# Value tiles of 125 or 128 rows, stored to DRAM and loaded again, in a decoder layer

## The chip, the cores and the metric

The kernel runs on one core of a Trainium2 chip. A core has five engines with instruction queues of their own: TensorE (PE), VectorE (DVE), ScalarE (ACT), GpSimd (POOL) and SyncE (SP), which here issues nearly all DMAs. They work on one on-chip memory of 128 partitions (SBUF, called `big` in this kernel) and wait for each other by semaphores. Transfers between SBUF and DRAM are carried out by 16 DMA engines. The metric is the time of one execution on the device in microseconds (us). The runs agree within about 0.3%.

## The reference

A decoder layer with pre-norm on a batch of 8 sequences of 112 tokens, width 512, and a context of 375 tokens per sequence:

```
x1  = x + self_attention(norm(x))                 16 heads of 32, rotary, causal mask
z   = ln(norm(x1))
S   = gqa(ln(q(z)), ln(k(z)), v(z))               16 query heads, 8 key/value heads of 128
X   = gqa(ln(qx(z)), ln(kx(ctx)), vx(ctx))        kx, vx: 512 -> 1024, from the 375 context tokens
x2  = x1 + fp8(concat(S, X)) @ wproj              inputs of q, k, v, qx and wproj rounded to fp8
h   = silu(gate(norm(x2))) * up(norm(x2))         2048 wide, ternary weights
out = x2 + rms_norm(h) @ w_proj                   ternary weights
```

The part that matters here is `vx(ctx)`: the values of the cross attention, for each of the 8 sequences a matrix of 375 x 1024. The 375 context tokens are worked on in three chunks of 125 tokens, and a chunk's tokens lie on 125 of the 128 partitions.

## The kernel before

The program has four layers of work that overlap: the first layer (self attention, up to about 200 us), two halves of the fp8 self attention (`S0`, `S1`), two halves of the cross attention (`X0`, `X1`, from 446 to 992 us), and the gated MLP. Each engine's order is written out by hand: a table of ticks (`A_PLAN` for the first layer, `ORDER` and `ORDER_X` for the rest) says which stage of which batch an engine issues at each tick. Every engine works strictly in that order, SP's DMA issues included.

To fill TensorE in the first layer, a part of the cross attention's work is done early. For each of 24 chunks of context (8 batches, 3 chunks each; `v_ld`, `v_in`) the split into two bf16 parts is made, and the result is stored to DRAM as `cs` (`v_cs`). For the first chunk of each batch (`EARLY = (0,)`) the value product is made as well, in two halves `h` of 512 columns: `v_mm` on TensorE (L1071), the copy out of PSUM into `v_out[h]` on ACT (`v_ev`, L1363), and the store from there to DRAM as `vs` (`v_st` on SP, L989). That makes 16 stores of 125 rows of 2 KB. `v_out[h]` is free again for the next copy when its store has landed.

On SP these stores stand between others: `cs` stores (L983), loads of context and of weights into one of four staging buffers (L941; `in_w_s` are the weights of the `S` halves, each load 512 KB over 128 rows), and the first layer's sum of a batch, which goes to DRAM and comes back in other rows (`xs`, L959 and L968). ACT takes a staged weight when it has landed (`b_0`, L1465).

In the cross attention, each of 16 steps (two halves, 8 batches) loads its value tile from `vs` into `vX[b % 2]` (`p_mm` on SP, L1018), as soon as the attention of the batch two before it is finished. The products of the attention weights with the values (`t_s3`, L1205) wait for it. They contract over 125 rows.

Lines that the text below names: on ACT L1397 the exponentials of the first layer and L1408 the copy of the transposed weights, L1503 the normalised projections; on VectorE L1744 the scaled output of a batch's attention; on TensorE L1059 the first layer's projections, L1121 its products with the values, L1081, L1109 and L1093 transposes and masks, L1144 and L1151 the projections of the halves.

Of the kernel before, what the change touches and what calls it, by code (L numbers as in the profile page):

```python
# [16 lines left out]
CK = 125  # L17
# [134 lines left out]
EARLY = (0,)  # L152
# [234 lines left out]
def _program(nc, ctx, x, ctx_t, w_a, w_s, w_x, w_v, w_p, w_g, w_d, vec, bias, cst, cst2, scr, xs, cs, vs, out):  # L387
# [4 lines left out]
    def sem(name):  # L392
        return ctx.enter_context(nc.semaphore(name))

    def signal(name, *stages, if_=None, each=None):

        keys = [k for s, k in steps["table"] if s in stages and (if_ is None or if_(k))]
        return Signal(sem("s_" + name), keys if each is None else [(k, e) for k in keys for e in each])

    def f32(a, n):  # L400
        return big[:, a:a + n]
# [79 lines left out]
    v_out = [f32(early.take(512), 512) for _ in range(2)]  # L481
# [12 lines left out]
    vX = [f32(a, 1536).rearrange("p (c n) -> p c n", c=3) for a in (X_V0, X_V1)]  # L494
# [24 lines left out]
    def unit(u):  # L519

        name, i = u
        n, c = divmod(i, 4)
        if name == "F":
            src = w_g[n // 2, :, n % 2, :] if n < 8 else w_d[n - 8]
            return src[:, 1024 * (c // 2):1024 * (c // 2) + 1024], None, None, None
        src, psrc = {"S": w_s, "X": w_x}[name[0]][int(name[1])], w_p[HALVES.index(name)]
        rows = src[n] if n < 4 else psrc[n - 4]
        rows = rows[:, 1024 * (c // 2):1024 * (c // 2) + 1024]
        if n >= 4:
            h = 4 * (n - 4) + c  # L530
            return rows, wp_half[name][:, 0, h, :], wp_half[name][:, 1, h, :], None
        sl = slice(512 * c, 512 * c + 512)
        v = ((0, 1, 2) if name[0] == "S" else (3, None, None))[max(0, c - 1)]
        scale = None if v is None else wsc[:, 4 * v + n:4 * v + n + 1]
        return rows, w_half[name][:, 0, n, sl], w_half[name][:, 1, n, sl], scale
# [6 lines left out]
    def spilled(u):  # L542
        return u[0] == "F" and u[1] >= FFN_DIRECT
# [22 lines left out]
    def att_no(h, b, g=3, e=1):  # L566
        return ATT.index((h, b, g, None if h[0] == "S" else e))
# [8 lines left out]
    def is_v(n):  # L576
        return PROJ[n][2] == "v"

    def proj_before(h, b):

        if b:
            return last_no(h, b - 1, "kv")
        return last_no("X0", NB - 1, "kv") if h == "X1" else proj_no("S1", NB - 1, "v", 0)

    def x_free(h, b, last):

        nb = NB * (h == "X1") + b
        if nb == 0:
            return [p_sum[proj_no("S1", NB - 1, "v", 0)]]
        if nb == 1:  # L590
            return [pv[att_no("S1", NB - 1)]]
        hb = divmod(nb - 2, NB)
        return [last[att_no(HALVES[2 + hb[0]], hb[1])]]
# [22 lines left out]
    s_vs = [Signal(sem(f"s_vs{i}"), [k for k in V_MADE if k[1] == i], 16) for i in range(2)]  # L616
    x_batches = [(h, b) for h in HALVES[2:] for b in range(NB)]
    s_ctx = Signal(sem("s_ctx"), x_batches, 16)
    s_vx = [Signal(sem(f"s_vx{i}"), [k for k in x_batches if k[1] % 2 == i], 16) for i in range(2)]
# [85 lines left out]


    pool_step = Steps(sem("s_pool_step"))
    rotated = signal("rotated", "a_rot")
    negmean = signal("negmean", "p_rstd", if_=lambda n: not is_v(n))
    q_made = Signal(sem("s_q_made"), quants("POOL", "t_s4"))  # L710
# [221 lines left out]
    def ps(user):  # L932
        return psum[bank.of[user]][:, :]

    def sync_program(e):
        w = Waits(e)

        def stage_load(user, n, src):
            for free in stage.after[user]:
                w.wait_ge(*free)  # L940
            e.dma_start(stage_buf[stage.of[user]][:, 0:n], src).then_inc(s_st[stage.of[user]], 16)  # L941

        def prep_a(c):
            for k in range(4):
                e.dma_start(wa_in[4 * c + k], w_a[k, :, 768 * c:768 * c + 768]).then_inc(s_wa[4 * c + k].sem, 16)
            if c == 0:
                e.dma_start(x1[0:T, 1, :], x[1]).then_inc(s_x[1].sem, 16)
                return
            e.dma_start(a_bias[0:T, :], bias).then_inc(s_bias.sem, 16)
            e.dma_start(vc, vec).then_inc(s_vec.sem, 16)  # L950
            e.dma_start(ck, cst2).then_inc(s_vec.sem, 16)
            for b in range(2, NB):
                e.dma_start(x1[0:T, b, :], x[b]).then_inc(s_x[b].sem, 16)

        def a_s4(g):
            b = g // 4
            if g % 4 == 3:
                w.wait_ge(*x1_made[g])
                e.dma_start(xs_rows[T * b:T * b + T, :], x1[0:T, b, :]).then_inc(s_xs[b].sem, 16)  # L959

        def l_h(b):
            i = b - 1
            if b:
                w.wait_ge(*s_xs[i]["out"])
                w.wait_ge(*s_xs[b]["out"])
                w.wait_ge(*stats["l_ln", i])
                w.wait_ge(*zl_made[i])
                e.dma_start(x1t[:, i, :], xs_rows[128 * i:128 * i + 128, :]).then_inc(s_xl[i].sem, 16)  # L968

        def b_0(u):  # L970
            if u[1] % 2 == 0:
                stage_load(u, 1024, unit(u)[0])

        def v_w(i):
            if i % 2 == 0:
                stage_load(("v_w", i), 1024, w_v[i // 2])

        def v_ld(m):
            stage_load(("v_ld", m), 1000, ctx_t[m])

        def v_cs(n):
            w.wait_ge(*chunk_lo[n])
            e.dma_start(cs[n // 3, :, n % 3, :], chunk_words[V_BUF[n]]).then_inc(  # L983
                s_cs[V_BUF[n]].sem, 16)

        def v_st(k):
            n, h = k
            w.wait_ge(*v_made[k])
            e.dma_start(vs[h, n // 3, :, EARLY.index(n % 3), :], v_out[h][0:CK, :]).then_inc(s_vs[h].sem, 16)  # L989

        def b_4(u):
            if spilled(u):
                w.wait_ge(*t_made[u])
                e.dma_start(scr[u[1] - FFN_DIRECT], spill_buf[spill_slot.of[u]]).then_inc(spill_out[u][0], 16)

        def b_back(_):
            for i in range(4):
                w.wait_ge(s_sp[i], 16 * sp_nth[i])
            w.wait_ge(*p_out[att_no("X0", 7)])
            for j in range(N_BACK):  # L1000
                e.dma_start(f32(PW[1] + 256 * (FFN_DIRECT + 4 * j), 1024).rearrange("p (u w) -> p u w", u=4),
                            scr[4 * j:4 * j + 4].rearrange("u p w -> p u w")).then_inc(s_back.sem, 16)

        def p_mm(n):
            h, b, what, c = PROJ[n]
            if h[0] == "S":
                return
            if (what, c) == ("q", 0):
                for s in s_cs:
                    w.wait_ge(*s[max(s.value)])  # L1010
                w.wait_ge(*p_sum[proj_before(h, b)])
                e.dma_start(ctx_words, cs[b].rearrange("p c w -> p (c w)")).then_inc(s_ctx.sem, 16)
            if (what, c) == ("k", 2):
                for s in s_vs:
                    w.wait_ge(*s[max(s.value)])
                for free in x_free(h, b, pv):
                    w.wait_ge(*free)
                e.dma_start(vX[b % 2][0:CK, 0:len(EARLY), :], vs[int(h[1]), b]).then_inc(s_vx[b % 2].sem, 16)  # L1018

        def d_1(b):  # L1020
            w.wait_ge(*y_out[b])
            e.dma_start(out_rows[128 * b:128 * b + 128, :], x1t[:, b, :]).then_inc(s_out.sem, 16)

        mine = dict(prep_a=prep_a, a_s4=a_s4, l_h=l_h, b_0=b_0, b_4=b_4, b_back=b_back, p_mm=p_mm, d_1=d_1,
                    v_w=v_w, v_ld=v_ld, v_cs=v_cs, v_st=v_st)
        for s, k in steps["SP"]:
            if s in mine:
                mine[s](k)
        e.wait_ge(*s_out[NB - 2])
# [274 lines left out]
    def scalar_program(e):  # L1304
        w = Waits(e)
# [51 lines left out]
        def v_ev(k):  # L1357
            n, h = k
            w.wait_ge(*v_sum[n, h, 2])
            before = V_MADE.index(k) - 2  # L1360
            if before >= 0:
                w.wait_ge(*s_vs[h][V_MADE[before]])
            e.activation(v_out[h][0:CK, :], ps(("v_mm", k))[0:CK, :], ACT.Copy).then_inc(v_made.sem, 1)  # L1363

        def a_rstd(b):
# [639 lines left out]
    def gpsimd_program(e):  # L2005
        w = Waits(e)
# [97 lines left out]
            e.tensor_tensor(sm[:, 1:2], sm[:, 0:1], cf[:, C_HALF:C_HALF + 1], ALU.pow).then_inc(f_rstd.sem, 1)  # L2104

        mine = dict(a_rot=a_rot, l_q=l_q, b_1=b_1, b_2=b_2, p_rstd=p_rstd, t_s4=t_s4, g_1=g_1, d_0=d_0)
        for s, k in steps["POOL"]:
            if s in mine:
                mine[s](k)
# [7 lines left out]
    @block.gpsimd  # L2117
    def _(eng):
        gpsimd_program(eng)
# [87 lines left out]
```

## Time and profile before

| | us |
|---|---|
| median of 3 runs | 1171.3 |
| lowest, highest | 1168.83, 1171.52 |
| the profiled execution | 1172.57 |
| its span in the profile | 1170.8 |

| engine | busy us | share of the span |
|---|---|---|
| TensorE | 1128.7 | 96% |
| VectorE | 836.1 | 71% |
| ScalarE | 795.0 | 68% |
| GpSimd | 608.4 | 52% |

The profile is one execution, recorded by the hardware. It tells for each instruction when it ran, which idle time of its engine lay ahead of it and what most likely ended that idle time (the releaser). The span is the time from the first to the last instruction; the execution's own time has 1.8 us more around it. "DMA share" is the mean busy share of the 16 DMA engines over a stretch: 1.00 is all sixteen at work. "PEclk" is the granted TensorE clock over a stretch, as a share of full speed. The mean over the whole span is 0.991.

### The profile page before, as it was taken

To read this page: it belongs to the slowest core of one execution; us is meant where nothing else is said; L and a number is where in the kernel's file an instruction comes from. 1 tells how busy PE (TensorE), PEld (TensorE's weight loads), DVE (VectorE), ACT (ScalarE), POOL (GpSimd) and SP (SyncE) were. 2 spreads that over 40 slices of the span, in tenths; PEclk is the share of its full clock that TensorE was granted. 3 is DMA by queue.
4 is the path that set the end of the run, shared out by engine and by line. 5 is a ranking of instruction groups with operands and counts; after the bars stand their busy time and mean duration, and the time that the engine had idled before them with its cause. 6 is when DMAs were issued, how large, how long until landed. Compare 5 with 4: busy or idle time off the path is not lost.

```text
span 1170.8 us, 20518 instructions
## 1 busy us (share of the span) xinstructions
PE 1128.7 (96%) x6269; PEld 766.3 (65%) x6330; DVE 836.1 (71%) x2761; ACT 795.0 (68%) x2348; POOL 608.4 (52%) x761
## 2 busy tenths in 40 slices
PE   5899999979999999999999999999999999999998
PEld 3576676756777776667667667667766767554564
DVE  5767997899877886668778776757776686676242
ACT  5665766888887887667777666667867678675130
POOL 1543885586454456526366464535545462356172
PEclk9999999999999999999999999999999999999999
DMA  9435433232211113023322223221341210000000
GB/s 283 161 110 177 132 111 100 67 107 73 73 55 37 38 55 108 30 96 108 117 85 77 83 88 99 72 81 37 119 139 56 90 37 10 1 1 1 36 1 27
DMA packets 36205, 92.98 MB, mean 79 GB/s; under 512 B 3568, under 2 KB 13936, under 8 KB 36096
## 3 DMA queue, kind: packets, MB, share of 16 engines
q1 hardware_dynamic: 35824, 91.30, 23.9%
q8 instruction: 51, 0.84, 0.3%
q14 instruction: 58, 0.48, 0.1%
q10 hardware_dynamic: 272, 0.36, 0.1%
HBM read 74.07 MB, written 17.58 MB: 78 GB/s over the span
## 4 chain that ended last, share of the span: by engine, by line
PE 84%; DVE 5%; DMA 4%; ACT 3%; issue 2%; SPq 1%; POOL 1%; ACTq 0%; DVEq 0%
PE ps L1151 17%; PE ps L1144 12%; PE ps L1205 8%; PE ps L1250 8%; PE ps L1221 8%; PE ps L1177 7%; PE ps L1186 4%; PE ps L1262 4%; PE ps L1163 4%; PE ps L1059 3%; DMA big<-in_w_s 2%; PE ps L1174 2%; PE ps L1071 2%; DMA big<-in_w_v 1%; PE ps L1121 1%
## 5 line engine op out<-in xcount | busy, mean ns | idle before, releaser
L1151 PE MATMUL ps<-big 128*125 128x512 bf16 x960 | 220.4, 379 | 0.0
L1503 ACT ACTIVATE big<-ps,big 112x128 f32<-112x128 f32 (+1 forms) x512 | 193.5, 465 | 15.3 <-POOL big L2061 14.5
L1144 PE MATMUL ps<-big 128*112 128x512 bf16 x768 | 187.5, 388 | 6.6 <-DVE big L1886 6.2
L1151 PEld LDWEIGHTS ps<-big 128*125 128x125 bf16 x960 | 127.5, 136 | 64.2
L1635 DVE BATCH_NORM_STATS2 big<-ps 112x6 f32<-112x128 f32 (+1 forms) x512 | 113.4, 284 | 43.9 <-PE ps L1151 28.7
L1144 PEld LDWEIGHTS ps<-big 128*112 128x112 bf16 x768 | 98.1, 132 | 60.2 <-DVE big L1886 6.8
L2058 POOL TENSOR_SCALAR big<-big 112x4 f32<-112x4 f32 (+1 forms) x128 | 46.3, 361 | 144.8 <-DVE big L1643 144.5
L1205 PE MATMUL ps<-big 125*128 125x224 f32 (+1 forms) x512 | 118.5, 353 | 1.2
L2071 POOL TENSOR_TENSOR big<-big 128x448 f32<-128x448 bf16 x64 | 62.8, 981 | 108.0 <-DVE big L1927 107.8
L1562 ACT ACTIVATE big<-ps 125x336 f32<-125x336 f32 x96 | 43.5, 453 | 103.1 <-PE ps L1186 102.6
L1205 PEld LDWEIGHTS ps<-big 125*128 125x128 f32 (+1 forms) x512 | 96.1, 191 | 13.1 <-issue 0.4
L1538 ACT ACTIVATE big<-ps,big 128x448 f32<-128x448 f32 (+1 forms) x128 | 95.0, 742 | 13.0 <-PE ps L1163 13.0
L1177 PE MATMUL ps<-big 128*112 128x375 f32 x256 | 101.7, 478 | 0.1
L1553 ACT ACTIVATE big<-ps,big 112x375 f32<-112x375 f32 x128 | 73.0, 570 | 42.2 <-DVE big L1846 42.2
L1846 DVE TENSOR_REDUCE big<-ps 112x1 f32<-112x375 f32 x128 | 68.8, 538 | 45.8 <-PE ps L1177 45.6
L1250 PE MATMUL ps<-big 128*128 128x512 bf16 (+1 forms) x505 | 98.6, 352 | 0.4
L1221 PE MATMUL ps<-big 128*128 128x512 bf16 x423 | 96.0, 379 | 1.3
L1867 DVE TENSOR_SCALAR big<-big 112x112 f32<-112x112 f32 (+1 forms) x256 | 94.9, 392 | 2.6 <-PE ps L1186 1.9
L2061 POOL TENSOR_TENSOR big<-big 112x4 f32<-112x4 f32 (+1 forms) x128 | 47.2, 369 | 82.1 <-ACT big L1314 78.2
L1186 PE MATMUL ps<-big 112*125 112x112 f32 (+1 forms) x512 | 84.3, 266 | 0.0
L1186 PEld LDWEIGHTS ps<-big 112*125 112x125 f32 (+1 forms) x512 | 73.0, 174 | 17.1 <-issue 0.4
L1250 PEld LDWEIGHTS ps<-big 128*128 128x128 bf16 x512 | 50.1, 98 | 44.4
(128 smaller groups left out, 2406.6 us busy)
## 6 DMA issues: line engine op xcount, KB each, us to landing
big<-cs SPq DMA_DIRECT2D x16, 750.0 KB, 4.2
big<-in_w_s SPq DMA_DIRECT2D x16, 512.0 KB, 4.3
big<-in_w_p SPq DMA_DIRECT2D x16, 512.0 KB, 5.2
big<-in_w_x SPq DMA_DIRECT2D x16, 512.0 KB, 3.8
big<-in_w_g SPq DMA_DIRECT2D x16, 512.0 KB, 5.3
big<-in_ctx_t SPq DMA_DIRECT2D x12, 500.0 KB, 7.1
cs<-big SPq DMA_DIRECT2D x24, 250.0 KB, 3.6
big<-in_w_d SPq DMA_DIRECT2D x8, 512.0 KB, 5.0
```

Of the source, the lines that this page charges most:

```text
L1144: t = e.matmul(bk[0:T, :], xq[:, k, :], wt[:, s, k, col:col + 512], start=k == s == 0, stop=k == 3 and s == 1)
L1151: t = e.matmul(bk[0:CK, :], ctxT[:, c, s, k, :], wt[:, u, k, col:col + 512], start=k == s == u == 0, stop=k == 3 and s == 1)
L1177: t = e.matmul(bk[0:T, 0:SC], q_sb[i][:, 2 * g + one, :], kX[i][:, g, :], start=True, stop=True)
L1186: t = e.transpose(bk[0:rows, T * j:T * j + T], p[0:T, rows * j:rows * j + rows], identf[0:T, 0:T])
L1205: t = e.matmul(ps(user)[:, o:o + 224], v[0:rows, c, 128 * g:128 * g + 128], pt[0:rows, 224 * c:224 * c + 224], start=c == 0, stop=S or c == 2)
L1221: t = e.matmul(bk, cat[:, k, :], wp_half[h][:, s, k, :], start=k == s == 0, stop=k == 7 and s == 1)
L1250: t = e.matmul(bk[:, 0:wide], wg[:, kk, 2048 * which + 128 * m:2048 * which + 128 * m + 128], xT[:, s, kk, n0:n0 + wide], start=kk == s == ...
L1503: t = e.activation(z[0:rows, 128 * j:128 * j + 128], ps(("p_mm", n))[0:rows, 128 * j:128 * j + 128], ACT.Identity, bias=v["q"][:, j:j + 1] ...
L1538: e.activation(dst, ps(("p_t", n))[:, 0:4 * rows].rearrange("p (g t) -> p g t", g=4), ACT.Identity, bias=bs, scale=wt).then_inc(qk_sb.sem, 1)
L1553: t = e.activation(p[0:T, 0:SC], bk[0:T, 0:SC], ACT.Exp, bias=sm[0:T, 0:1], accum_out=sm[0:T, 2:3])
L1635: t = e.bn_stats(v["st"][:, j, :], src[0:rows, width * j:width * j + width])
L1867: t = e.tensor_scalar(dst, src, ri[:, j:j + 1], None, ALU.mult)
```

## The change

The value tiles are stored and loaded as 128 rows in place of 125. The DRAM tensor `vs` gets 128 rows for each tile. GpSimd sets both buffers `v_out[0]` and `v_out[1]` to zero once, before all its other work, and signals it (`v_clear`). ACT waits for that signal ahead of its copy, which still writes rows 0 to 124, so rows 125 to 127 stay zero in every tile that is stored. The load writes all 128 rows of `vX`, and the products still read 125 of them. No other instruction is added, removed or moved.

```diff
--- before.py
+++ after.py
@@ -705,6 +705,7 @@
 
 
     pool_step = Steps(sem("s_pool_step"))
+    v_clear = Signal(sem("s_v_clear"), range(2))
     rotated = signal("rotated", "a_rot")
     negmean = signal("negmean", "p_rstd", if_=lambda n: not is_v(n))
     q_made = Signal(sem("s_q_made"), quants("POOL", "t_s4"))
@@ -986,7 +987,7 @@
         def v_st(k):
             n, h = k
             w.wait_ge(*v_made[k])
-            e.dma_start(vs[h, n // 3, :, EARLY.index(n % 3), :], v_out[h][0:CK, :]).then_inc(s_vs[h].sem, 16)
+            e.dma_start(vs[h, n // 3, :, EARLY.index(n % 3), :], v_out[h]).then_inc(s_vs[h].sem, 16)
 
         def b_4(u):
             if spilled(u):
@@ -1015,7 +1016,7 @@
                     w.wait_ge(*s[max(s.value)])
                 for free in x_free(h, b, pv):
                     w.wait_ge(*free)
-                e.dma_start(vX[b % 2][0:CK, 0:len(EARLY), :], vs[int(h[1]), b]).then_inc(s_vx[b % 2].sem, 16)
+                e.dma_start(vX[b % 2][:, 0:len(EARLY), :], vs[int(h[1]), b]).then_inc(s_vx[b % 2].sem, 16)
 
         def d_1(b):
             w.wait_ge(*y_out[b])
@@ -1360,6 +1361,7 @@
             before = V_MADE.index(k) - 2
             if before >= 0:
                 w.wait_ge(*s_vs[h][V_MADE[before]])
+            w.wait_ge(*v_clear[h])
             e.activation(v_out[h][0:CK, :], ps(("v_mm", k))[0:CK, :], ACT.Copy).then_inc(v_made.sem, 1)
 
         def a_rstd(b):
@@ -2104,6 +2106,9 @@
             e.tensor_tensor(sm[:, 1:2], sm[:, 0:1], cf[:, C_HALF:C_HALF + 1], ALU.pow).then_inc(f_rstd.sem, 1)
 
         mine = dict(a_rot=a_rot, l_q=l_q, b_1=b_1, b_2=b_2, p_rstd=p_rstd, t_s4=t_s4, g_1=g_1, d_0=d_0)
+
+        for h in range(2):
+            e.memset(v_out[h], 0.0).then_inc(v_clear.sem, 1)
         for s, k in steps["POOL"]:
             if s in mine:
                 mine[s](k)
@@ -2200,7 +2205,7 @@
     scr = nc.dram_tensor("scr", (36, 128, 256), mb.dt.float32, kind="Internal").ap()
     xs = nc.dram_tensor("xs", (896, 512), mb.dt.float32, kind="Internal").ap()
     cs = nc.dram_tensor("cs", (8, 128, 3, 500), mb.dt.float32, kind="Internal").ap()
-    vs = nc.dram_tensor("vs", (2, 8, 125, len(EARLY), 512), mb.dt.float32, kind="Internal").ap()
+    vs = nc.dram_tensor("vs", (2, 8, 128, len(EARLY), 512), mb.dt.float32, kind="Internal").ap()
     decoder_layer(nc, *args, scr, xs, cs, vs, out)
     r = run(nc, [{"in_" + k: v for k, v in arrays.items()}], core_ids=[0])
     return r.results[0]["out_0"]
```

The only engine whose order changes is GpSimd. Its first rows before (`big` is SBUF; the TENSOR_TENSOR rows are the rotation of queries and keys in the first layer):

```order
L2196 MEMSET const-float32-1.0 128x1
L2196 MEMSET const-bfloat16-1.0 128x1
L2196 MEMSET const-uint8-127 128x1
L2117 UNCONDITIONAL_BRANCH
L2018 ISA
L2018 TENSOR_TENSOR big<-big 112x512
L2020 TENSOR_TENSOR big<-big 112x512
L2023 TENSOR_TENSOR big<-big 112x512
```

The same place in the changed kernel (line numbers are some lines higher):

```order
L2201 MEMSET const-float32-1.0 128x1
L2201 MEMSET const-bfloat16-1.0 128x1
L2201 MEMSET const-uint8-127 128x1
L2122 UNCONDITIONAL_BRANCH
L2111 MEMSET big 128x512 x2
L2020 ISA
L2020 TENSOR_TENSOR big<-big 112x512
L2022 TENSOR_TENSOR big<-big 112x512
L2025 TENSOR_TENSOR big<-big 112x512
```

Two memsets of 128x512 now stand ahead of the first rotation; all rows behind them keep their order.

## Rows read from the trace of the kernel before

**Rows 1.** the page: busy time of the engines, and the chain that ended last

```profile
PE 1128.7 (96%) x6269; PEld 766.3 (65%) x6330; DVE 836.1 (71%) x2761; ACT 795.0 (68%) x2348; POOL 608.4 (52%) x761
...
PE 84%; DVE 5%; DMA 4%; ACT 3%; issue 2%; SPq 1%; POOL 1%; ACTq 0%; DVEq 0%
```

**Rows 2.** busy time by stage: stretch, length, each engine, TensorE clock, DMA share, GB/s

```profile
60.00:130.00 70.00, 65.77 (x453) 46.87 (x452) 50.71 (x87) 47.03 (x166) 34.28 (x26) 1.00 0.43 140
130.00:200.00 70.00, 69.78 (x495) 50.56 (x493) 59.32 (x121) 43.82 (x164) 55.06 (x46) 1.00 0.37 114
446.00:992.00 546.00, 543.90 (x2805) 381.81 (x2841) 393.19 (x1484) 392.35 (x1099) 275.87 (x378) 1.00 0.25 82
```

**Rows 3.** DMA issues by line, with landing; and the instructions that touch `vs`

```profile
vs<-big SPq DMA_DIRECT2D x16, 250.0 KB
...
cs<-big SPq DMA_DIRECT2D x24, 250.0 KB, 3.6
...
L989 SPq DMA_DIRECT2D vs<-big x16: 255/332/894, 59.8 to 204.9; - x16
...
L1018 SPq DMA_DIRECT2D big<-vs x16: 270/271/300, 446.0 to 980.5; - x16
```

**Rows 4.** narrow stretches: last store alone, a `cs` store, before a landing

```profile
205.30:208.30 3.00, 3.00 (x31) 2.38 (x30) 1.27 (x3) 2.58 (x8) 0.20 (x1) 0.82 0.32 101
146.00:147.00 1.00, 1.00 (x7) 0.58 (x5) 0.96 (x2) 1.00 (x8) 1.00 (x2) 1.00 0.81 278
123.00:124.00 1.00, 1.00 (x6) 0.60 (x5) 0.97 (x3) 0.12 (x1) 0.92 (x2) 1.00 0.34 133
```

**Rows 5.** SP's queue, 86 to 114 us: start, length, line, what is issued

```profile
86.98 0.33 SPq L989 DMA_DIRECT2D vs<-big  x1
...
87.79 0.65 SPq L941 DMA_DIRECT2D big<-in_w_s  x1
...
110.58 0.38 SPq L941 DMA_DIRECT2D big<-in_w_s  x1
...
111.95 0.39 SPq L989 DMA_DIRECT2D vs<-big  x1
...
113.83 2.87 SPq L941 DMA_DIRECT2D big<-in_w_s  x1
```

**Rows 6.** ACT timeline: its waits for `in_w_s`, idle time and releaser in brackets

```profile
82.81 0.72 ACT L1465 ACTIVATE big<-big 128x512 bf16<-128x512 f32 x1 [3.82 <-DMA big<-in_w_s]
...
96.22 0.72 ACT L1465 ACTIVATE big<-big 128x512 bf16<-128x512 f32 x1 [3.97 <-DMA big<-in_w_s]
...
114.74 0.72 ACT L1465 ACTIVATE big<-big 128x512 bf16<-128x512 f32 x1 [3.94 <-DMA big<-in_w_s]
...
123.88 0.72 ACT L1465 ACTIVATE big<-big 128x512 bf16<-128x512 f32 x1 [2.33 <-DMA big<-in_w_s]
```

**Rows 7.** TensorE timeline: the instructions with idle time before them, 96 to 214 us

```profile
100.79 0.57 PE L1081 MATMUL ps<-big 112*128 112x112 f32 x4 [1.06 <-ACT big L1397]
...
107.09 0.60 PE L1109 MATMUL ps<-big 112*112 112x112 f32 x4 [0.94 <-DVE big L1744]
...
116.86 2.15 PE L1059 MATMUL ps<-big 128*112 128x512 bf16 x9 [0.87 <-ACT big L1397]
...
120.35 0.56 PE L1093 MATMUL ps<-big 112*112 112x448 bf16 x2 [0.57 <-ACT big L1397]
...
129.42 0.85 PE L1059 MATMUL ps<-big 128*112 128x512 bf16 x3 [0.78 <-ACT big L1408]
...
200.96 0.97 PE L1121 MATMUL ps<-big 112*112 112x32 f32 x8 [1.17 <-ACT big L1503]
```

**Rows 8.** VectorE timeline: L1744 of the batch that ends at 107 us

```profile
106.34 0.69 DVE L1744 TENSOR_TENSOR big<-ps,big 112x512 f32<-112x512 f32 x1
```

**Rows 9.** GpSimd timeline: its first work after the start

```profile
24.14 1.27 POOL L2018 TENSOR_TENSOR big<-big 112x512 f32<-112x512 f32 x1 [23.72 <-DVE big L1706]
```

**Rows 10.** busy time and granted clock after the gap at 200.96

```profile
200.00:210.00 10.00, 9.04 (x60) 6.61 (x61) 6.69 (x22) 9.50 (x36) 2.35 (x4) 0.83 0.34 103
```

## The prediction

> **What bounds the kernel now.** I read the page first: the busy line of the engines and the chain that ended last. TensorE is busy for 96% of the span and holds 84% of the chain; DMA holds 4% [rows 1]. TensorE runs its instructions in a fixed order, so a DMA can be worth time only where it leaves TensorE idle. I then asked for busy time by stage. In the first layer, where the value tiles are stored, TensorE idles 4.23 us between 60 and 130 us and 0.22 us between 130 and 200 us. In the cross-attention stages, where the tiles are loaded again, it idles 2.1 us out of 546 [rows 2].
>
> Next come the issues of the two transfers that change: 16 stores `vs<-big` and 16 loads `big<-vs`, 250 KB each. The view gives no landing time for them, though it gives one for other issues [rows 3]. So I cut a stretch of 3 us out of the last store, issued at 204.9 us with nothing behind it. The mean busy share of the 16 DMA engines is 0.32 [rows 4]. Five engines of sixteen would be 0.31. A `cs` store of the same size, with 128 rows, shows 0.81 in the stretch in which it runs [rows 4]. My reading: the 125-row transfer uses five DMA engines, and the 128-row transfer uses all sixteen.
>
> That alone does no harm, since nothing waits for the value store. The harm is to what is queued behind it. The ACT timeline shows four waits for `in_w_s`, a weight load: 3.82, 3.97, 3.94 and 2.33 us [rows 6]. SP's queue shows what was issued ahead of each [rows 5]. The load that ended the second wait was issued at 87.79 us, right behind the value store of 86.98. The one that ended the fourth wait was issued at 113.83, behind the store of 111.95. The third waited for the load issued at 110.58, ahead of the value store of its group. So did the first: in its group, too, SP issues the weight load first and the value store behind it. Just before the fourth wait ended, at 123 to 124 us, the DMA share was 0.34 [rows 4]: again about five engines finishing, with the other eleven done. So two of the four waits stand behind a five-engine store.
>
> **The change part by part.**
>
> The transfer itself. From 205.3 to 208.3 us the lone store took 0.32 x 3 x 16 = 15.4 us of DMA-engine time [rows 4]. On five engines that is 3.1 us each, on sixteen 0.96 us each. With 128/125 of the rows it is 0.99. A transfer behind it that needs all sixteen engines therefore lands about 2.1 us earlier. The bounds are 0 (the landing is set by the late engines' other work) and 3.1 us (the whole store out of the way).
>
> The Trainium skill, page "DMA: Bandwidth & Descriptors", section "Why a DMA increments its semaphore by 16 and not by 1", says that a DMA runs on the largest number of engines up to 16 that divides the slowest dimension of both sides; that is 5 for 125 rows and 16 for 128. By that rule, the trace agrees for before (share 0.31), and the changed store must use all sixteen.
>
> What the 2.1 us is worth. The two ACT waits shrink from 3.97 to 1.9 us and from 2.33 to 0.2 us. TensorE sees it only in its own gaps, five between 100 and 130 us: 1.06, 0.94, 0.87, 0.57 and 0.78 us, 4.22 us together [rows 7].
> - The gap of 1.06 us (100.79) ends with the exponentials of ACT, which ACT runs in the 4.6 us after the second wait (over at 96.22). ACT 2.1 us earlier is more than 1.06: the gap goes, -1.06.
> - The gap of 0.94 us (107.09) ends with VectorE's L1744, which needs the last products of TensorE. TensorE stopped at 106.15, VectorE began at 106.34 and took 0.69 [rows 8]. VectorE comes from the same delayed ACT work, so at most the 0.2 us of lateness goes and the operation stays: -0.1, bounds 0 and -0.2.
> - The gaps of 0.87 and 0.57 us follow the third ACT wait. That load is issued once a batch's sum has been stored, which follows TensorE. It moves with TensorE and the gaps stay: 0, bounds 0 and -1.44.
> - The gap of 0.78 us (129.42) ends with an ACT copy, 5.5 us after the fourth wait was over (123.88). That wait shrinks by 2.1: -0.78.
> Sum: -1.06 - 0.1 - 0.78 = -1.94, rounded -2.0 us. What is late next is VectorE at 107 us and the third weight load; both follow TensorE. After 130 us TensorE is full until 200 us, so an earlier TensorE carries the 2 us forward.
>
> The stretch that follows has its own gap, 1.17 us at 200.96 behind ACT's L1503 [rows 7]. That work begins only after TensorE's last first-layer projections, so it moves along: 0, bounds 0 and -1.17.
>
> The loads. Sixteen loads, five engines before, sixteen after, each with 0.96 us of queue time in place of 3.1. TensorE idles only 2.1 us in this whole stage [rows 2] and no wait there names this load: 0. The cover is the double buffer: a load goes out when the batch two before it is done, a whole batch ahead of its use, and a batch takes (980.5 - 446.0) / 15 = 36 us [rows 3]. Without that cover each load would have cost up to its 3.1 us.
>
> The two memsets (128x512, fp32, GpSimd) stand ahead of its first instruction, which waits until 24.14 us. The nearest operation is that instruction itself, 112x512 with two inputs, at 1.27 us [rows 9]. Two of them are 2.6 us at most, inside an idle stretch of 23.7 us: 0. ACT's new wait is for a signal given ahead of GpSimd's work at 24 us, and the first value tile is stored at 59.8 us [rows 3]; ACT's queue behind it never stands: 0. The three more rows add 6 KB to each of 32 transfers: 0. If the memsets were not covered, they would cost their 2.6 us once.
>
> The profiled execution took 1172.57 us (span 1170.8), so by the sum 1170.6. It lies 1.3 us above the median of the runs, 1171.3; from the median the sum gives **1169.3 us**.
>
> **The rivals.**
>
> *No relief.* The late engines may be late for another reason: the queue holds several large transfers at those moments, and even the first wait, with its store issued behind it, is as long (3.82 us) as the second. Then the landings stay, and the time is 1171.3. Against it: the share of about 0.3 just ahead of the landing at 123.9. The form in which the change does not do what it says (the store still on five engines) gives the same time.
>
> *Much more.* All five gaps go (4.22), the gap at 200.96 goes too (1.17), and the granted clock no longer falls behind it. The clock stood at 0.83 over 200 to 210 us [rows 10], a mean of the full 2.4 GHz and the half level of 1.2 GHz; that is 0.17 x 10 = 1.7 us at most. Together 7.1 us: 1164.2. For it: the chain that ended last gives DMA 4% of the span, 47 us, far more than all of TensorE's gaps here. Against it: the third wait has no value store ahead, and the gap at 200.96 lies behind TensorE's own work.
>
> *Slower: the clock falls somewhere new.* The clock fell after TensorE's gap of 1.17 us at 200.96, but it stayed at 1.00 over 60 to 130 us, with gaps of up to 1.06 [rows 2, 7]. If a moved gap meets the clock's control less luckily, each new fall costs the 1.7 us worked out above. One cancels most of the gain; this is slower than before from two, and with three and the gain of 2.0 the time is 1171.3 - 2.0 + 5.1 = 1174.4. For it: the gaps at 100 to 130 us are nearly as long as the one that brought the fall. Against it: the change makes gaps smaller, not longer. The Trainium skill, page "TensorE: Matmul & The Clock Gate", Part 1, says that the monitor runs freely, so the same kernel meets it at another point each run. By that rule part of the spread of the three runs (1168.8 to 1171.5) is such falls; no row here shows it.
>
> **How the numbers follow.** My forecast has 0.54, no relief 0.20, much more 0.18, slower by the clock 0.08. The first two lie within 0.3% (3.5 us, about what a measurement of this kernel can tell from no change), save a small part of the forecast's upper side that reaches past 3.5 us when the gaps of the third wait go as well (2.0 + 1.44 = 3.4, with a further tenth from the second gap). So faster 0.22, within 0.3% 0.71, slower 0.07. The range goes from 1165.0, near the case of much more, to 1172.6, the unchanged time with some of one clock fall.
>
> **What would show it.** In the changed profile the value stores and loads have a landing time, near the 3.6 us of the `cs` store; the narrow stretches over the last store show a share near 0.8 for about 1 us instead of 0.31 for 3. ACT's waits for `in_w_s` fall from 14 us to about 10 us in the first layer, by the second and the fourth. TensorE's gaps between 60 and 130 us fall from 4.2 to about 2.3 us, with those at 100.8 and 129.4 gone and those at 107 and 117 to 120 still there. The stages from 446 us on are unchanged. The forecast is wrong if the ACT waits keep their length (no relief), if the gaps behind the third wait close as well (much more), or if the granted clock is below 1.00 in a stretch between 60 and 200 us (slower).

## The result, and the profile after

| | before | after |
|---|---|---|
| median of 12 runs, us | 1169.32 | 1166.86 |
| lowest, highest | 1168.42, 1172.42 | 1165.55, 1168.89 |
| the profiled execution | 1172.57 | 1166.84 |

The change makes the kernel 2.5 us faster: ratio 0.9977, 95% interval 0.9970 to 0.9985. The forecast was 2.0 us faster from the median then known, 1171.3, so 1169.3 us. That median came from three runs, of which two lay in the upper part of what the kernel does; over 12 runs it is 1169.3. So the time that was forecast is what the kernel takes without the change. The measured 1166.9 lies 2.4 us below it, inside the stated range of 1165.0 to 1172.6.

The waits for DMA in the first layer, 60 to 215 us of the changed kernel (engine, line, what was waited for, us in total, times, longest), and below it the same for each wait on ACT:

```profile
ACT big L1467 <- DMA big<-in_w_s: 7.1, 3, 4.2
```

```profile
81.60 0.72 ACT L1467 ACTIVATE big<-big 128x512 bf16<-128x512 f32 x1 [2.50 <-DMA big<-in_w_s]
...
91.83 0.72 ACT L1467 ACTIVATE big<-big 128x512 bf16<-128x512 f32 x1 [0.47 <-DMA big<-in_w_s]
...
109.69 0.72 ACT L1467 ACTIVATE big<-big 128x512 bf16<-128x512 f32 x1 [4.15 <-DMA big<-in_w_s]
```

These answer to [rows 6]. The second wait fell from 3.97 to 0.47 us and the fourth is gone (but see the experiments: the fourth is not in every profile with 125 rows either). The third, with no value store ahead of it, stayed (3.94 and 4.15). SP's queue of the changed kernel around the second and the third load:

```profile
85.76 0.43 SPq L990 DMA_DIRECT2D vs<-big  x1
...
86.73 0.46 SPq L942 DMA_DIRECT2D big<-in_w_s  x1
...
102.60 0.32 SPq L960 DMA_DIRECT2D xs<-big  x1
...
105.32 0.38 SPq L942 DMA_DIRECT2D big<-in_w_s  x1
```

The load issued at 86.73 had landed when ACT went on at 91.83, 5.1 us later. Before, it took from 87.79 to 96.22, 8.4 us [rows 5, 6]. TensorE by stage, and the last value store (issued at 199.6 us):

```profile
60.00:130.00 70.00, 70.00 (x498) 51.06 (x497) 54.87 (x96) 51.20 (x178) 40.29 (x29) 1.00 0.44 146
60.00:215.00 155.00, 153.79 (x1091) 112.38 (x1090) 123.77 (x256) 108.18 (x394) 100.63 (x83) 0.99 0.37 122
446.00:992.00 546.00, 545.93 (x2835) 380.78 (x2834) 390.41 (x1466) 386.73 (x1087) 271.47 (x371) 1.00 0.24 78
199.90:201.90 2.00, 2.00 (x19) 1.42 (x19) 0.62 (x1) 1.97 (x7) 0.20 (x1) 0.93 0.34 131
200.50:201.00 0.50, 0.50 (x6) 0.50 (x5) 0.00 (x0) 0.50 (x2) 0.20 (x1) 1.00 1.00 385
```

TensorE has no idle time left between 60 and 130 us, where it had 4.23 [rows 2]. The last store is over within the 2 us, at a mean share of 0.34. While it runs, the share is 1.00: all sixteen engines.

The stretch that [rows 4] gives for the kernel before is not the last store alone, as it is called there. At 101 GB/s its 3 us moved 303 KB (KB as 1000 bytes), and one store of 125 rows holds 256. Part of what was issued before it was still under way, and SP had issued another value store 3.5 us earlier:

```profile
201.42 0.26 SPq L989 DMA_DIRECT2D vs<-big  x1
...
204.87 0.26 SPq L989 DMA_DIRECT2D vs<-big  x1
```

The last load of a value tile, issued at 980.54 us, is a 125-row transfer that does stand alone:

```profile
981.40:984.40 3.00, 3.00 (x19) 2.18 (x18) 1.56 (x6) 2.87 (x10) 0.41 (x2) 1.00 0.29 85
```

It moved 255 KB, one tile, in this stretch, so five engines of sixteen (0.31) for just under 3 us. The reading of five engines stands; its price is worked out anew below. The issues by line, which answer to [rows 3], now have a landing time for both transfers:

```profile
big<-in_ctx_t SPq DMA_DIRECT2D x12, 500.0 KB, 4.9
cs<-big SPq DMA_DIRECT2D x24, 250.0 KB, 2.6
vs<-big SPq DMA_DIRECT2D x16, 256.0 KB, 2.6
big<-vs SPq DMA_DIRECT2D x16, 256.0 KB, 2.7
```

The `cs` stores, which the change does not touch, land in 2.6 us in place of 3.6, and the loads of context in 4.9 in place of 7.1. They shared the queue with the five-engine stores. Over all 16 loads of `in_w_s` the median from issue to landing stays at 4.3 us, so most of them gain nothing.

### The profile page after: what moved, and what is told of

It is laid out like the page before. It is cut to its first block, busy times and chain, and to the rows that moved or that the text cites. A ratio compares the mean times of both kernels' runs of the same rounds, so it can differ in the third digit from the quotient of the medians.

```text
span 1165.0 us, 20583 instructions
## 1 busy us (share of the span) xinstructions
PE 1130.7 (97%) x6330; PEld 767.1 (66%) x6330; DVE 834.8 (72%) x2761; ACT 791.4 (68%) x2348; POOL 611.4 (52%) x763
## 4 chain that ended last, share of the span: by engine, by line
PE 90%; DVE 5%; DMA 1%; POOL 1%; issue 1%; SPq 1%; ACT 1%; ACTq 0%; DVEq 0%
PE ps L1152 18%; PE ps L1145 12%; PE ps L1251 8%; PE ps L1222 8%; PE ps L1206 8%; PE ps L1178 7%; PE ps L1060 4%; PE ps L1187 4%; PE ps L1164 4%; PE ps L1263 4%; PE ps L1072 3%; PE ps L1175 2%; PE ps L1122 2%; PE ps L1100 1%; DMA big<-in_w_v 1%
## 5 line engine op out<-in xcount | busy, mean ns | idle before, releaser
L1222 PE MATMUL ps<-big 128*128 128x512 bf16 x448 | 101.3, 379 | 0.0
L1164 PEld LDWEIGHTS ps<-big 112*128 112x128 f32 (+1 forms) x512 | 60.3, 142 | 29.5 <-issue 13.6
```

What stands on the lines that cost most here:

```text
L1164: t = e.transpose(bk[:, rows * j:rows * j + rows], z[0:rows, 128 * j:128 * j + 128], identf[0:rows, 0:rows])
L1222: t = e.matmul(bk, cat[:, k, :], wp_half[h][:, s, k, :], start=k == s == 0, stop=k == 7 and s == 1)
```

## The experiments

All ratios are to the kernel before on the same chip. In the code excerpts `-` is what the edit takes away; the ends of lines (`.then_inc(...)`) and the semaphore counts that go with a second DMA are left out.

**The kernel before, once more.** 

> The kernel before, once more, as a measure of its own spread and with a second profile. The change's median gain is 2.5 us, but the two profiled executions differ by 5.7 us (1172.57 and 1166.84). Theory A (the profiled execution of before was a slow one of its kind): this one lies near 1169.3 us, with less idle time of TensorE between 60 and 130 us than the 4.2 us of the first profile, or fewer falls of the clock. Theory B (the first profile is typical and the medians hide it): again about 4.2 us idle there and a time near 1172. Ratio to before 1.000 within 0.1% by both.

Measured: 1169.8 us, ratio 0.9999 (0.9990 to 1.0008). Its profiled execution took 1168.94 us. Its ACT waits and its TensorE by stage:

```profile
81.84 0.72 ACT L1465 ACTIVATE big<-big 128x512 bf16<-128x512 f32 x1 [2.58 <-DMA big<-in_w_s]
...
95.04 0.72 ACT L1465 ACTIVATE big<-big 128x512 bf16<-128x512 f32 x1 [3.53 <-DMA big<-in_w_s]
...
112.33 0.72 ACT L1465 ACTIVATE big<-big 128x512 bf16<-128x512 f32 x1 [3.95 <-DMA big<-in_w_s]
...
120.59 0.72 ACT L1465 ACTIVATE big<-big 128x512 bf16<-128x512 f32 x1 [1.47 <-DMA big<-in_w_s]
```

```profile
60.00:130.00 70.00, 68.64 (x489) 49.79 (x488) 52.97 (x90) 48.53 (x173) 36.91 (x28) 1.00 0.45 142
60.00:215.00 155.00, 151.70 (x1076) 109.69 (x1075) 122.93 (x247) 107.06 (x390) 99.25 (x81) 1.00 0.39 121
446.00:992.00 546.00, 545.91 (x2836) 380.72 (x2835) 390.56 (x1468) 388.23 (x1089) 273.72 (x375) 1.00 0.24 79
```

The four waits are there again, but TensorE idles 1.36 us between 60 and 130 us in place of 4.23. Theory A holds: the first profile has more idle time than this one. It also had a fall of the granted clock behind the gap at 200.96 (0.83 over 200 to 210 us, [rows 10]) that this one does not have, though the same gap is there:

```profile
198.53 0.97 PE L1121 MATMUL ps<-big 112*112 112x32 f32 x8 [1.18 <-ACT big L1503]
```

```profile
200.00:210.00 10.00, 9.66 (x77) 7.12 (x76) 7.91 (x28) 9.16 (x36) 7.12 (x8) 1.00 0.27 77
```

TensorE comes to this gap 2.4 us earlier than in the first profile, and from it to the gap in front of L1109 that both profiles have (222.67 and 219.12) it takes 20.6 us in place of 21.7. These two, 2.4 and 1.1 us, are nearly all of the 3.6 us between the two executions.

The third row of the stages corrects another reading. The first profile's 2.1 us of idle time in the cross attention [rows 2] goes with 2805 matmuls in place of 2836, while its weight loads are all there (2841): these were missing records, not idle time.

**The memsets and the wait alone**, with 125 rows. 

> The two memsets and ACT's wait for them alone; stores and loads of 125 rows as before. My theory (they are covered by GpSimd's idle stretch up to 24 us): no change, ratio 1.000 within 0.1%. Rival (a part of the gain or a loss comes from the start, or from a shift of the work against the clock): 1 us or more either way. ACT's waits for in_w_s stay as they were.

Measured: 1170.2 us, ratio 1.0001 (0.9992 to 1.0010). The memsets cost nothing and bring nothing, to within the 1.2 us of the interval. In the profile of this kernel, and in that of the loads in two pieces below, ACT's fourth wait for `in_w_s` is missing, although the stores have 125 rows. So its absence in the changed kernel can't be put down to the change.

**The stores alone**, on the changed kernel: its stores of 128 rows, with loads of 125.

```diff
-e.dma_start(vX[b % 2][:, 0:len(EARLY), :], vs[int(h[1]), b])
+e.dma_start(vX[b % 2][0:CK, 0:len(EARLY), :], vs[int(h[1]), b, 0:CK])
```

> The change with its stores of 128 rows, but loads of 125 rows. My theory (all of the gain comes from the stores, by what is queued behind them in the first layer): the whole gain, 2.5 us, ratio 0.998, and TensorE idle under 0.5 us between 60 and 130 us. Rival (the loads carry part of it, in the 546 us of the cross attention, where the changed profile has 2 us less idle): about 1 us of the 2.5 is missing, ratio 0.999.

Measured: 1167.1 us, ratio 0.9976 (0.9966 to 0.9985), the whole gain. TensorE's idle time from 60 to 130 us is 0.67 us, a little over what was expected; the section on the prediction comes back to this.

**The loads alone, in two pieces**, on the kernel before.

```diff
-e.dma_start(vX[b % 2][0:CK, 0:len(EARLY), :], vs[int(h[1]), b])
+for lo, hi in ((0, 112), (112, CK)):
+    e.dma_start(vX[b % 2][lo:hi, 0:len(EARLY), :], vs[int(h[1]), b, lo:hi])
```

> The kernel before with each load of 125 rows issued as two, of 112 and 13 rows, so that 16 and 13 DMA engines share the work in place of five; stores as before. My theory (the loads are hidden by a whole batch): no change, ratio 1.000 within 0.1%. Rival (the loads carry part of the gain): about 1 us faster.

Measured: 1169.9 us, ratio 1.0000 (0.9991 to 1.0009). The loads were hidden, and faster loads are worth nothing that the 1.1 us of the interval would show.

**127 rows**, on the changed kernel, with loads of 125.

```diff
-e.dma_start(vs[h, n // 3, :, EARLY.index(n % 3), :], v_out[h])
+e.dma_start(vs[h, n // 3, 0:127, EARLY.index(n % 3), :], v_out[h][0:127, :])
```

> The change with stores of 127 rows in place of 128 (loads of 125 rows). 127 has no divisor from 2 to 16. My theory (the number of DMA engines of a store sets what it costs those behind it; one engine by the divisor rule): the lone store is at a share near 0.06 for 11 us and more, the in_w_s loads behind stores land 8 us and more late, TensorE idles 10 us or more between 60 and 200 us, and the time rises by 10 to 60 us. Rival (what helped is only that the rows reach nearly all of the 128 partitions, or the number of rows): 127 is as good as 128, about 1167.

Measured: 1228.6 us, ratio 1.0495 (1.0481 to 1.0508). That is 58 us over the kernel before, at the top of what was expected, and one row less than the change costs 61 us more than it. A window behind the last store but one (issued at 253.7 us), and its waits for DMA from 60 to 215 us:

```profile
255.00:262.00 7.00, 5.39 (x46) 3.93 (x45) 4.87 (x17) 3.21 (x14) 2.15 (x3) 1.00 0.07 26
```

```profile
ACT big L1467 <- DMA big<-in_w_s: 34.7, 5, 9.7
ACT big L1355 <- DMA cs<-big: 19.3, 3, 7.7
ACT big L1365 <- DMA vs<-big: 10.8, 2, 6.3
```

A share of 0.07 is one engine of sixteen (0.06). ACT now waits longer for weights, for `cs` stores (L1355), and for the value store itself (L1365).

**126 rows**, by the same edits with 126. 

> Stores of 126 rows (loads of 125): 14 DMA engines with 9 rows each by the divisor rule, between the five of 125 rows and the 16 of 128. My theory (the number of engines decides, not whole tiles and not more rows): as good as 128 within 0.5 us, ratio 0.998, against 127 rows that were 58 us slower. Rival (only the full 128 partitions give the gain): near 1.000 or worse.

Measured: 1167.4 us, ratio 0.9965 (0.9952 to 0.9977); the changed kernel beside it had 0.9976 (0.9966 to 0.9986). So 125, 126, 127 and 128 rows give 1170, 1167, 1229 and 1167 us. Neither full tiles nor the bytes order them. The rows show five engines for 125 rows (share 0.29 to 0.32), one for 127 (0.07) and sixteen for 128 (1.00). For 126 rows, half a microsecond of the last store:

```profile
200.60:201.10 0.50, 0.50 (x7) 0.49 (x6) 0.38 (x1) 0.50 (x2) 0.35 (x1) 1.00 0.87 270
```

Fourteen of sixteen would be 0.88. The Trainium skill, page "DMA: Bandwidth & Descriptors", section "Why a DMA increments its semaphore by 16 and not by 1", gives the largest divisor up to 16: 5, 14, 1 and 16 engines. By that rule, the trace agrees for all four shares, and the order of the four times follows the number of engines, with no difference that can be told between 14 and 16.

**125 rows in two stores**, of 112 and 13 rows, on the kernel before, with no memset and no zero rows.

```diff
-e.dma_start(vs[h, n // 3, :, EARLY.index(n % 3), :], v_out[h][0:CK, :])
+for lo, hi in ((0, 112), (112, CK)):
+    e.dma_start(vs[h, n // 3, lo:hi, EARLY.index(n % 3), :], v_out[h][lo:hi, :])
```

> The kernel before with each store of 125 rows issued as two, of 112 and 13 rows (16 and 13 DMA engines by the divisor rule), no memset, no zero rows, loads of 125 rows. My theory: the same gain as the change, 2 to 2.5 us, less up to 0.5 us for 16 more issues of 0.33 us on SP. Rival (the gain needs whole tiles of 128 rows, or comes from something else in the change): no gain, 1169.3.

Measured: 1168.3 us, ratio 0.9978 (0.9970 to 0.9987); the changed kernel beside it had 0.9970 (0.9961 to 0.9979). The gain comes without the three rows. The two ratios differ by less than their intervals.

**The five-engine stores behind the loads**, on the kernel before. SP holds a value store back until the loads of context and weights of its tick are issued.

```diff
 for s, k in steps["SP"]:
+    if s == "v_st":
+        held.append(k)
+        continue
+    if held and (s in ("v_cs", "b_4", "b_back", "d_1") or (s == "a_s4" and k % 4 == 3)):
+        for one in held:
+            v_st(one)
+        held = []
```

> The kernel before with its 125-row stores on five engines, but issued behind the loads of context and weights of the same tick, so that the two in_w_s loads that ended ACT's long waits are ahead of a store in the queue. My theory (the harm is only to what is queued behind a store): those waits shrink as with the change, TensorE idle between 60 and 130 us falls under 1 us, 1.5 to 2.5 us faster. Rival (a five-engine store harms what is in flight beside it too, or the next transfer behind it is as critical): 0 to 1 us faster.

Measured: 1169.0 us, ratio 0.9986 (0.9978 to 0.9995), about 1.6 us faster, where the changed kernel beside it had 0.9970 (0.9961 to 0.9979). That is the low end of what was expected and about half of what the change brings here, so the rival is right in part. ACT's waits show why:

```profile
92.49 0.72 ACT L1473 ACTIVATE big<-big 128x512 bf16<-128x512 f32 x1 [0.65 <-DMA big<-in_w_s]
...
95.85 0.62 ACT L1362 ACTIVATE big<-big 128x500 bf16<-128x500 f32 x1 [2.63 <-DMA cs<-big]
```

The second wait for weights shrank as with the change, with the store still on five engines: what counts for it is what is ahead in the queue. But a `cs` store then stood behind the value store, and ACT waited 2.63 us for that one. TensorE's idle time from 60 to 130 us is 1.08 us, where under 1 us was expected.

**The changed kernel again, twice.** Both are the changed kernel as it stands. 

> The changed kernel itself, once more, beside the three others on the same chip: 2.5 us faster than before, ratio 0.998, and a second profile of it, with TensorE idle under 0.5 us between 60 and 130 us.

> The changed kernel once more on the same chip, for comparison with the three others: ratio 0.997 to 0.998 to the kernel before, TensorE busy for all of 60 to 130 us.

Measured: 1167.2 and 1167.9 us, ratios 0.9970 (0.9961 to 0.9979) and 0.9976 (0.9966 to 0.9986). TensorE is busy for 70.00 of 70 us from 60 to 130 us in both profiles.

**The changed kernel with its stores behind the loads.** 

> The changed kernel with its 128-row stores issued behind the loads of context and weights of the same tick. With five engines that order was worth 1.6 us, since the wait moved from in_w_s to a cs store behind. My theory (a 128-row store costs those behind it about 1 us of queue and no wait of TensorE hangs on that any more): as the changed kernel, within 0.5 us. Rival (what is left of ACT's second wait, 0.5 us, still costs): 0.5 us faster than it; or slower, if the stores' landing now holds up the next copies.

Measured: 1167.2 us, ratio 0.9965 (0.9952 to 0.9977). No difference from the changed kernel (0.9976, 0.9966 to 0.9986) can be told, which leaves room for the rival's 0.5 us.

**Seven eighths of the value stores left out.** Each store has 16 rows, and the loads fetch 128 rows of a weight in their place, so the kernel leaves out the values themselves. 

> The changed kernel with 7/8 of the value stores left out: 16 rows of a tile are stored, and the loads fetch 128 rows of a weight in its place. It bounds what any better store could bring. My theory (TensorE has no idle time left in 60 to 130 us that hangs on the stores): as the changed kernel, within 0.5 us. Rival (the stores' bytes still hold up the weights): 1 us faster or more.

Measured: 1166.9 us, ratio 0.9965 (0.9952 to 0.9977), again as the changed kernel. Nothing that could be measured is left to win at these stores, and no version here beats the changed kernel beyond the intervals.

## Why the prediction was right, step by step

*The bottleneck and the cause: right.* Everything comes from the stores (the stores alone have the whole gain), nothing that can be measured from the loads or the memsets, and the number of DMA engines is the cause, as the four numbers of rows and the store in two pieces show. The rival of no relief falls with that.

*The clock: no net loss, but a sign that was named came.* The mean granted clock was 0.991 before and 0.990 after. The prediction called a granted clock below 1.00 between 60 and 200 us a sign against it. It came: 0.98 over 130 to 200 us, because TensorE's gap of 1.2 us, and the fall of the clock behind it, now stand at 195 us. The fall moved with the gap; it did not multiply. It is not tied to the change. The gap is there, with 1.17 to 1.19 us, in all thirteen profiles other than the one of 127 rows. In six of them the clock fell within the 10 us behind it, and in seven it stayed at 1.00, with both outcomes among the profiles of the kernel before and among those of the changed kernel. The prediction had no row for such chance; these are some. It priced a fall at 1.7 us. From this gap to the one in front of L1109 TensorE takes 21.7 us with a fall and 20.6 without, for the kernel before and for the changed one alike: 1.1 us.

*The 2.1 us of relief: too small, and the right difference from a wrong stretch.* From its issue to ACT's start, the second weight load took 8.4 us in the first profile and 8.2 us in the second (86.80 to 95.04) of before, and 5.1 us after. That is 3.1 to 3.3 us, the upper bound of that term. The prediction took 15.4 us of engine time for one store out of a stretch that moved more than one store. The transfers that do stand alone took 0.29 x 3 x 16 = 13.9 us of engine time with 125 rows (a load, not a store), 2.8 us for each of five engines, and 0.34 x 2 x 16 = 10.9 us with 128 rows, 0.7 us for each of sixteen. The difference is 2.1 us again, by luck. So 1.0 to 1.2 us of what was measured stay unexplained.

*The waits: right in kind for the second.* It shrank from 3.97 and 3.53 us in the two profiles of before to 0.47, and the third stayed. All waits together fell from 14.1 to 7.1 us, where about 10 was forecast. The first shrank as well against the first profile (3.82 to 2.50), but it was 2.58 in the second profile of before, so this is no effect of the change. Nor is the end of the fourth shown to be one, as said above.

*The gaps: the step that failed.* The prediction let VectorE's L1744 wait for the TensorE products that ended at 106.15, priced the gap behind it at -0.1 with a bound of -0.2, and let the third weight load move with TensorE, so that the two gaps behind it (116.86 and 120.35) would stay, at 0. "If the gaps behind the third wait close as well" was its own sign of being wrong, and they closed. TensorE's gaps in this stretch, in us, named by their place in the first profile (the three profiles of the changed kernel have none):

| gap | before | before, again | memsets alone | loads in two | stores alone |
|---|---|---|---|---|---|
| 100.79 | 1.06 | | 0.59 | | |
| 107.09 | 0.94 | | | 0.78 | |
| 116.86 | 0.87 | 0.69 | 0.94 | 1.20 | |
| 120.35 | 0.57 | 0.55 | 0.55 | 0.56 | 0.55 |
| 129.42 | 0.78 | | | | |

The gaps that the prediction closed, at 100.79 and 129.42, come and go: over the first four profiles, those with the five-engine stores in their old place, they make 0.6 us on average. The pair that it left standing is in all four, with 1.5 us on average.

Why the pair closes, the changed kernel shows. L1744 (now L1746) here, on VectorE:

```profile
100.14 0.69 DVE L1746 TENSOR_TENSOR big<-ps,big 112x512 f32<-112x512 f32 x1
```

and TensorE's products and transposes:

```profile
104.02 0.88 PE L1122 MATMUL ps<-big 112*112 112x32 f32 x8
104.74 0.57 PE L1110 MATMUL ps<-big 112*112 112x112 f32 x4
```

L1746 ran 4 us ahead of those products, so it never needed them; it scales a batch whose products were done earlier. What held it up at 106.34 in [rows 8] is VectorE's own queue, which stood behind ACT's split of a context chunk (L1354), and ACT had waited for the weights and then for a `cs` store. ACT's line, and VectorE's share of the split before and after:

```profile
102.39 1.13 ACT L1354 ACTIVATE big<-big 128x500 bf16<-128x500 f32 x2 [0.43 <-DMA cs<-big]
```

```profile
103.05 3.10 DVE L1683 TENSOR_TENSOR big<-big 128x500 bf16<-128x500 f32 x2 [1.11 <-ACT big L1354]
```

```profile
98.69 1.25 DVE L1685 TENSOR_TENSOR big<-big 128x500 bf16<-128x500 f32 x2
```

VectorE began 4.4 us earlier, as ACT did (96.22 to 91.83), and its two instructions took 1.25 us in place of 3.10. Together that is the 6.2 us by which L1746 came earlier. The store of the batch's sum, which waits for what follows L1746, went from 107.84 to 102.60, and the third load from 110.58 to 105.32: 5.3 us earlier, while TensorE's position had moved by 2.4 us (the transposes at 107.09 in [rows 7] stand at 104.74). The third wait is as long as before, but it lies 2.7 us earlier against TensorE's work, and all gaps behind it closed. That is the part that the prediction had given to the rival of much more.

The step from 3.10 to 1.25 us is one that neither the prediction nor an experiment aimed at, and it goes with the pair of gaps without exception. In seven profiles (the four above, the stores alone, the store in two pieces, the five-engine stores behind the loads) the two instructions took 2.4 to 3.4 us, and the gap at 120.35 is there. In six (the three of the changed kernel, 126 rows, the changed kernel with its stores behind, the one with stores of 16 rows) they took 1.3 us, and there is none. What differs is which operation of GpSimd runs beside them. Before:

```profile
102.66 1.27 POOL L2018 TENSOR_TENSOR big<-big 112x512 f32<-112x512 f32 x1
103.89 1.72 POOL L2020 TENSOR_TENSOR big<-big 112x512 f32<-112x512 f32 x1
```

and after:

```profile
98.53 2.27 POOL L2036 TENSOR_TENSOR big<-big 128x448 bf16<-128x448 f32 x1
```

L2036 took 2.27 us beside them, and 1.00 us (as L2034) in the kernel before, where it ran ahead of them. In the seven profiles VectorE had waited 0.55 to 1.50 us for ACT's split just before the two instructions, in the six not at all. So a wait of half a microsecond was followed by 1.2 to 2.1 us more, and these pass on to the third load. The stores alone, whose first layer is the same as the changed kernel's, came out on the long side: ACT had waited 1.02 us for a `cs` store there, and VectorE 0.85 us for ACT. That the two engines slow each other is read off these coincidences; no run isolates it.

*The sum: right by luck.* Against the first profile the steps gave 1.94 us where 4.2 of idle time went. But that profile had more idle time than most of its kernel. The same four profiles have 5.41, 3.30, 3.65 and 4.26 us idle from 60 to 215 us, 4.2 on average. The three of the changed kernel have 1.21, 1.21 and 1.58, and the stores alone 2.59, 1.7 on average. The difference of 2.5 us agrees with the 2.5 us of the medians. So errors cancelled: the relief was too small, the gaps that it closed stood mostly in that one execution, and those that carry the gain were left out.

What stays open is why one and the same first layer comes out on one side or the other, at VectorE and at the clock, why the idle time of the kernel before varies from 3.3 to 5.4 us, and 1.0 to 1.2 us of the second load's relief. Nothing here isolates them.

## What to carry to other kernels

Look at the number of rows of every DMA before its bytes: 125 rows ran on five DMA engines and 127 on one, while 126 and 128 were as good as each other, and nothing need wait for the transfer itself for the harm to be real, since what is queued behind it lands late. A pad to 128 rows or a second issue for the odd rows does the same here. Before a gap is called safe because it "follows" another engine, find the operand that it really waits for: here a neighbour in time was taken for it. And take a second profile of the same kernel where effects are near 0.2%: here one profile gave as much weight to gaps that came and went as to those that stayed.

## What the runs showed of the hardware

The one-engine store was worse than its share tells. Sixteen stores at one engine each cost 61 us against the same stores on sixteen engines, some 3.8 us each, and five engines cost 2.5 us in all. A short delay can hide in slack where a long one does not; this is argued and not shown. A part is clock: the mean granted clock was 0.968 with 127 rows and 0.993 in the changed kernel on the same chip. By my estimate from these two, (1 - 0.968) x 1226.7 = 39 us against 0.007 x 1166.0 = 8 us, up to 31 of the 61 us are lost that way, less where TensorE was waiting anyway.

A gap of TensorE of one and the same length, 1.17 to 1.19 us at one and the same place, was followed by a stretch at the half clock in some executions of a kernel and not in others: 0.83 over 200 to 210 us in the first profile of before, 1.00 in the second.

The profile's count of matmuls is to be read beside idle time: 31 missing records of 2836 looked like 2.0 us of idle TensorE.
